# Reordering the mixes, the row factors and the last norm of a gated retention block on one core

## The chip, the cores and the metric

One NeuronCore of a Trainium2 chip runs the whole program. The metric is the device time of one execution in microseconds, lower is better. All tensors are float32; the large products run on fp32r operands that are split into a high and a low part.

## The reference, cut to what matters

The input x is (8, 1024, 128): eight sequences of 1024 tokens, 128 channels. A conditioning vector gives each sequence two scales, two shifts and two gates. A retention block (8 heads, keys of 64, values of 128, decay in place of a softmax) and then a token-shift feed-forward block are added to x.

```python
mod = (_silu(L0_c) @ L0_wmod).reshape(L0_c.shape[0], 6, 1, -1)
sa, ca, ga, sb, cb, gb = (mod[:, 0], mod[:, 1], mod[:, 2], mod[:, 3], mod[:, 4], mod[:, 5])
...
h = _layernorm(x, axis=-1) * (1 + ca) + sa
x = x + ga * _L0_attn_ref(h, ...)
h = _layernorm(x, axis=-1) * (1 + cb) + sb
x = x + gb * _L0_ffn_ref(h, ...)
return x
...
# in _L0_attn_ref: q, k rotated; scores times decay; then
o = jnp.einsum('bhts,bhsv->bhtv', scores, v)
o = (o - mean) * jax.lax.rsqrt(var + EPS)
o = o * gn_weight.reshape(H, V) + gn_bias.reshape(H, V)
o = o * jax.nn.silu(g)
return jnp.einsum('btc,oc->bto', o, Wo)
...
# in _L0_ffn_ref
xr = mu_r * x + (1.0 - mu_r) * x_prev
xk = mu_k * x + (1.0 - mu_k) * x_prev
r = jax.nn.sigmoid(jnp.einsum('btc,dc->btd', xr, W_r))
k_act = jnp.square(jax.nn.relu(jnp.einsum('btc,dc->btd', xk, W_k)))
out = r * jnp.einsum('btc,dc->btd', k_act, W_v)
```

## The kernel before, in words

The 8192 tokens are cut into 64 chunks of 128; four chunks are a group of 512 tokens, so there are 16 groups, numbered 0 to 15 (LAST is 15). Each engine has its own instruction stream, written out by hand: a prologue for the first chunks and then one loop over `steps`, in which every piece of work has an own offset (`due(step - 11, GC, LAST)` means: in step 11, 15, 19 and so on, for group 0, 1, 2). Inside an engine the order of the lines is the order of the work; between engines there are semaphores alone. The step numbers of different engines are not the same moment: VectorE's step t follows ScalarE's step t - 1.

One step carries one chunk through TensorE: `turn_heads` and `transpose_k`, `attend`, `scores`, `recall`, `state`, and projections of later chunks. TensorE's PSUM banks are a ring of five; a bank is taken only when the reader of its last content has released it, so TensorE waits for VectorE's products of rotated keys and queries (`sin_k`, `cos_q`), for the states (`S`) and for ScalarE's copies (`v`). `recall` ends a chunk's heads; ScalarE squares them (`square`, tile N), VectorE sums the squares (`sum_squares`, gn_sum), GpSimd makes 1/std (`head_rstd`, a power of -0.5), VectorE normalises (`norm_heads`), and the next `attend` but one needs the heads' banks free again. GpSimd also finishes the rotations (`rotate_k`, `rotate_q`) and multiplies two heads a step by their gates (`gate_head`, tile y).

Once in four steps, a group's work is added to that:
- From group 4 on (BY_ROWS) the first norm is made on the turned input: `apply_rows` (VectorE, line 1071) multiplies x_turned by the row factors 1/std and by the channel scale, and `add_rows` (GpSimd, line 1410) adds the row of shifts. Before, apply_rows stands between the two halves of `norm_heads`, and add_rows ahead of `rotate_k`.
- The feed-forward's token shift: `mix_delta` (GpSimd, line 1461) makes h minus its predecessor, `mix_shift_r` (line 1164) and `mix_shift_k` (line 1170, in place, tile delta) on VectorE make both mixes, and `round_mix` (ScalarE, line 847) the high part of mix k. Before, both mixes stand ahead of the masks of the scores (`mask`, line 1125), and round_mix is the last line of ScalarE's step.
- The norms' statistics: `norm_stats` (VectorE, lines 1051 and 1054) is four bn_stats and four bn_aggr; `norm_rstd` on GpSimd makes 1/std and the shift.

The end is written out for group 15 in two halves of 256 tokens: `last_residual`, `last_stats`, `last_rstd` (GpSimd), `last_apply` (ScalarE, line 864), `last_transpose` (TensorE, with `keep_busy` matmuls of no use ahead of each half), `last_modulate` (ScalarE, line 884), `last_mix` (VectorE, line 1232), `last_k`, `last_r`, `last_ffn` (TensorE), and `last_product`. GpSimd's last line is `ffn_out` of group 14, whose store SP waits for before it issues the last two.

Of the kernel before, what the change touches and what calls it, by code (L numbers as in the profile page):

```python
# [9 lines left out]
ALU = mybir.AluOpType  # L10
# [39 lines left out]
    "last_heads", "last_k_act", "last_k_psum", "last_mix_k", "last_mix_r", "last_mv", "last_n1T", "last_neg",  # L50
    "last_out", "last_product", "last_r_psum", "last_r_tanh", "last_relu", "last_residual", "last_rstd",
    "last_scaled", "last_shift", "last_stats", "last_var", "last_y", "ln_apply0", "ln_apply1", "ln_mv0",
# [39 lines left out]
def build(nc, x, xT, cT, w_mod, w_qkT, w_gT, w_vT, w_oT, norm_wb, w_ffnT, ffn_mu, const, const_q, out):  # L92
    with ExitStack() as ctx:
# [201 lines left out]
        def _(e):  # L295
# [427 lines left out]
        def _(e):  # L723
# [135 lines left out]
            def last_apply(part):  # L859
                at.wait_ge("last_shift", part + 1)  # L860
                at.wait_ge("n0T", BY_ROWS)
                at.wait_ge("n1T", LAST)
                for j in range(GC)[chunks_of(part)]:
                    e.activation(normed[:, j, :], X[:, LAST % NX, j, :], ACT.Identity, bias=ln_shift[:, 1, j:j + 1],
                                 scale=ln_rstd[:, 1, j:j + 1]).then_inc(sem["last_apply"])

# [83 lines left out]
            for step in steps:  # L950
                for i in due(step, 1, NCHUNK, 4):
                    square(i, 0)
                for i in due(step, 1, NCHUNK, 4):
                    square(i, 1)
                for g in due(step - 12, GC, LAST - 1):
                    act_r(g)
# [28 lines left out]
                for g in due(step - 9, GC, LAST):  # L985
                    round_mix(g)
# [5 lines left out]
            last_apply(0)  # L992
            last_modulate(0)
            last_apply(1)
            last_modulate(1)
            for part in range(PARTS):
                last_relu(part)
                last_act_r(part)

        @block.vector  # L1000
        def _(e):
# [42 lines left out]
            def norm_stats(g, which):  # L1044
# [4 lines left out]
                at.wait_ge(f"ln_shift{which}", g)  # L1049
                for j in range(GC):  # L1050
                    e.bn_stats(ln_stats[:, which, j, :], X[:, g % NX, j, :]).then_inc(sem[f"ln_stats{which}"])
                for j in range(GC):
                    at.wait_ge(f"ln_stats{which}", GC * g + j + 1)
                    done = e.bn_aggr(ln_mv[:, which, j, :], ln_stats[:, which, j, :])
# [152 lines left out]
            def last_stats(part):  # L1207
# [10 lines left out]
                at.wait_ge("last_mv", part + 1)  # L1218
                e.tensor_scalar(ln_neg[:, 1, these], ln_mv[:, 1, these, 0], -1.0, None, ALU.mult).then_inc(sem["last_neg"])

            def last_mix(part):
# [9 lines left out]
                for n, what in ((1, "k"), (0, "r")):  # L1231
                    e.scalar_tensor_tensor(out=last_mixed[what][:, cols], in0=last_delta[:, cols], scalar=mu[:, n:n + 1], in1=before,
                                           op0=ALU.mult, op1=ALU.add).then_inc(sem["last_mix_" + what])
# [17 lines left out]
            norm_stats(0, 0)  # L1251
            sum_w_v()
# [11 lines left out]
            norm_stats(1, 0)  # L1264
            mask(0, 1)
            mask(0, 0)
            add_state(0)
            rotate_k(2)
# [24 lines left out]
            norm_stats(3, 0)  # L1293
            norm_heads(2, 0)
# [9 lines left out]
            for step in steps:  # L1304
# [4 lines left out]
                for g in due(step + 10, GC, NGROUP, 4):  # L1309
                    norm_stats(g, 0)  # L1310
                for g in due(step - 11, GC, LAST):
# [3 lines left out]
                for g in due(step - 11, GC, LAST):  # L1315
                    mix_shift_k(g)
                for g in due(step - 9, GC, LAST):
                    norm_stats(g, 1)
                for i in due(step, 1, NCHUNK, 5):
# [376 lines left out]
```

## Time and profile before

| | us |
|---|---|
| three timed runs | 750.21, 751.33, 752.49 (median 751.33) |
| the profiled execution | 750.83 |
| its span, first to last instruction | 749.0 |
| TensorE busy | 735.4 |
| VectorE busy | 605.7 |
| GpSimd busy | 604.3 |
| ScalarE busy | 482.4 |

The profile is of one execution. Busy times of TensorE overlap a little, because matmuls are pipelined and their ends are modelled; a stall of TensorE is seen more exactly in the distance between the starts of two matmuls. A row of the timeline gives the start, the duration, engine, line and tiles, and in brackets how long the engine was idle before it and what it then waited for. Rows that follow one another closely are merged (x2).

### The profile page before, as it was taken

The numbers are of one execution on the slowest core, as the hardware profiler recorded it, in microseconds if no ns is written. First come the engines' busy times: TensorE is split into PE (matmuls) and PEld (weight loads), VectorE is DVE, ScalarE is ACT, GpSimd is POOL, SyncE is SP. The second block draws the span as 40 slices with busy tenths as digits, with TensorE's granted clock in tenths as the row PEclk, the third lists the DMA queues.
The fourth block names the chain that finished last, engine by engine and source line by source line (L and its number), as shares of the span: only waits on it lengthen the run. The fifth ranks groups of instructions, "written<-read, shape, count | busy, mean of one in ns | idle before, by whom it ended". The sixth has DMA issues, their size and how long they took to land.

```text
span 749.0 us, 29004 instructions
## 1 busy us (share of the span) xinstructions
PE 735.4 (98%) x12123; PEld 643.0 (86%) x12123; DVE 605.7 (81%) x1265; ACT 482.4 (64%) x932; POOL 604.3 (81%) x655
## 2 busy tenths in 40 slices
PE   8989999999999999999999999999999999999997
PEld 7778888888889889888888988988888888988886
DVE  4997688878888887988888898887898878787546
ACT  4566666575665666666666665766666666656665
POOL 5877779789698897988889797888979889787641
PEclk9999999999999999999999999999999999999999
DMA  7611020200202121030211303021020201001001
GB/s 249 193 31 20 13 59 10 65 18 16 79 17 79 25 73 30 10 93 13 75 25 26 81 13 87 9 79 31 13 84 17 73 16 30 18 9 31 24 15 29
DMA packets 59809, 35.15 MB, mean 47 GB/s; under 512 B 36664, under 2 KB 54432, under 8 KB 59680
## 3 DMA queue, kind: packets, MB, share of 16 engines
q1 hardware_dynamic: 58960, 32.51, 16.8%
q8 instruction: 96, 1.57, 0.9%
q10 hardware_dynamic: 720, 0.80, 0.3%
q14 instruction: 33, 0.27, 0.1%
HBM read 20.66 MB, written 4.25 MB: 33 GB/s over the span
## 4 chain that ended last, share of the span: by engine, by line
PE 81%; DVE 10%; issue 3%; ACT 2%; POOL 2%; DMA 1%; SPq 0%; DVEq 0%
PE ring L332 45%; PE outs L332 13%; PE O_E L332 12%; PE ring L347 7%; PE O_O L332 2%; DVE gn_sum L1145 2%; DVE N L1152 1%; DVE delta L1170 1%; ACT N L803 1%; DVE S L1139 1%; DMA N<-in_w_vT 1%; PE ring L397 1%; DVE mix_r L1164 1%; DVE rot_k L1115 1%; DVE sin_k L1118 1%
## 5 line engine op out<-in xcount | busy, mean ns | idle before, releaser
L1452 POOL TENSOR_TENSOR y<-y,gate 128x512 f32<-128x512 f32 x120 | 152.4, 1287 | 29.4 <-ACT y L815 29.4
L1435 POOL TENSOR_TENSOR rot_k<-rot_k,sin_k 128x256 f32<-128x256 f32 x128 | 106.2, 850 | 26.5 <-DVE sin_k L1118 25.8
L332 PEld LDWEIGHTS outs<-wo_gated,y 128*128 128x128 f32 x992 | 119.8, 192 | 6.7 <-DVE y L1191 0.5
L779 ACT ACTIVATE v<-ring 64x512 f32<-64x512 f32 x128 | 76.0, 594 | 75.3 <-PE ring L332 74.3
L332 PE MATMUL outs<-wo_gated,y 128*128 128x128 f32 x992 | 121.7, 275 | 0.1
L1145 DVE TENSOR_REDUCE gn_sum<-N 128x4 f32<-128x512 f32 x118 | 75.5, 681 | 43.4 <-ACT N L803 43.4
L1445 POOL TENSOR_TENSOR gn_rstd<-gn_var,minus_half 128x8 f32<-128x8 f32 x64 | 105.3, 1645 | 5.0
L787 ACT ACTIVATE kT<-ring 128x512 f32<-128x512 f32 x64 | 38.3, 598 | 103.0 <-PE ring L347 103.0
L815 ACT ACTIVATE y<-ring,gn 128x512 f32<-128x512 f32 x126 | 90.9, 777 | 5.2 <-PE ring L347 5.2
L1125 DVE TENSOR_TENSOR A<-ring,consts 128x256 f32<-128x256 f32 x128 | 48.2, 417 | 56.2 <-PE ring L332 56.2
L1429 POOL TENSOR_TENSOR qT<-qT,swapped 128x512 f32<-128x512 f32 x60 | 77.2, 1287 | 14.8 <-DVE swapped L1101 14.6
L808 ACT ACTIVATE gate<-ring 128x512 f32<-128x512 f32 x128 | 76.8, 601 | 3.6 <-PE ring L332 1.2
L1139 DVE TENSOR_TENSOR S<-ring,S 128x512 f32<-128x512 f32 x112 | 76.8, 685 | 2.9 <-PE ring L332 1.0
L332 PE MATMUL O_E<-v,A 64*64 64x128 f32 x992 | 68.0, 275 | 0.6 <-DVE N L1152 0.6
L332 PE MATMUL O_O<-v,A 64*64 64x128 f32 x992 | 68.0, 275 | 0.0
L332 PE MATMUL ring<-v,rot_k 64*64 64x128 f32 x960 | 67.5, 270 | 0.3 <-DVE A L1125 0.3
L332 PE MATMUL ring<-v,k_odd 64*64 64x128 f32 x960 | 67.1, 269 | 0.0
L332 PE MATMUL O_E<-S,qT 64*64 64x128 f32 x928 | 65.3, 269 | 0.1
L332 PE MATMUL O_O<-S,qT 64*64 64x128 f32 x928 | 64.6, 269 | 0.0
L332 PEld LDWEIGHTS ring<-v,rot_k 64*64 64x64 f32 x960 | 57.6, 133 | 0.8 <-issue 0.8
L332 PEld LDWEIGHTS ring<-v,k_odd 64*64 64x64 f32 x960 | 57.9, 133 | 0.0
L332 PEld LDWEIGHTS O_E<-v,A 64*64 64x64 f32 x992 | 53.1, 132 | 4.8 <-DVE N L1152 0.7
(199 smaller groups left out, 2107.9 us busy)
## 6 DMA issues: line engine op xcount, KB each, us to landing
k_odd<-rot_k SPq DMA_DIRECT2D x128, 64.0 KB, 2.2
row_of<-written_rows SPq DMA_DIRECT2D x12, 512.0 KB, 4.0
X<-in_x SPq DMA_DIRECT2D x16, 256.0 KB, 4.3
out<-X SPq DMA_DIRECT2D x15, 256.0 KB, 2.4
x_turned<-in_xT SPq DMA_DIRECT2D x12, 256.0 KB, 4.4
key_tables<-in_const SPq DMA_DIRECT2D x7, 256.0 KB, 5.1
rotary_q<-in_const_q SPq DMA_DIRECT2D x2, 512.0 KB, 6.4
gates<-stored_rows SPq DMA_DIRECT2D x8, 128.0 KB, 3.1
```

What stands on the lines that cost most here:

```text
L332: return e.matmul(o, lhsT, rhs, start=start, stop=stop, skip_group_check=True)
L347: done = e.transpose(bank[:, at_column:at_column + HALF], tokens[rows, :], ident[rows, rows])
L779: done = e.activation(v[halves(half), i % 2, 1, :, :], by(PAIRS, bank_of["v", odd, i][halves(1 - half), :]), ACT.Copy)
L808: e.activation(gate[:, n % 2, :], bank_of["gate", n][:, :], ACT.Silu).then_inc(sem["gate"])
L815: e.activation(in_halves(by(GC, y[:, n % NY, :])), from_halves(bank_of["n", n // 2], n % 2, GC), ACT.Identity, bias=gn[:, 1, h:h + 1], sca ...
L1125: e.tensor_tensor(A[:, odd, :, :], by(PAIRS, bank_of["kT", i][:, odd, W // 2:W]), causal.unsqueeze(1).broadcast_to([P, PAIRS, HALF]), ALU. ...
L1139: e.tensor_tensor(new, added, old, ALU.add).then_inc(sem["S"])
L1145: e.tensor_reduce(gn_sum[:, i % 2, odd, :], N[:, i % NN, odd, :, :], AXIS.X, ALU.add).then_inc(sem["sum_" + eo])
L1429: e.tensor_tensor(q, q, swapped[:, :], ALU.add).then_inc(sem["qT"])
L1435: done = e.tensor_tensor(turned[:, n, :, :], turned[:, n, :, :], sin[:, n, :, :], op)
L1445: e.tensor_tensor(gn_rstd[:, i % 2, :, :].rearrange("p e a -> p (e a)"), gn_var[:, i % 2, :, :].rearrange("p e a -> p (e a)"), minus_half[ ...
L1452: e.tensor_tensor(y[:, n % NY, :], y[:, n % NY, :], gate[:, n % 2, :], ALU.mult).then_inc(sem["y"])
```

## The change

- VectorE's `norm_stats` is cut into `norm_stats` (bn_stats) and `norm_mv` (bn_aggr). For group 2, in the prologue, the first part moves ahead of `rotate_k(2)`; both masks of chunk 2 move ahead of the second half of `norm_heads(0)`.
- In the loop, `mix_shift_k` and `apply_rows` move behind the masks, `round_mix` moves from the end of ScalarE's step to behind the squares of the next one, and GpSimd's `add_rows` moves between the two `gate_head`.
- At the end, `last_apply` moves from ScalarE to VectorE as (x - mean) * 1/std, so -mean and the shift are not made any more; mix k of both halves comes ahead of mix r; `last_k` of both halves comes first on TensorE, `last_relu` of both on ScalarE; the filler matmuls go from 5 and 4 to 2 and 3; `ffn_out` of group 14 moves from GpSimd to VectorE (`last_ffn_out`).

```diff
@@ TensorE
             at.wait_ge("n_O", NCHUNK)
-            keep_busy(O[1][:, :, :].rearrange("p n v -> p (n v)"), 5, True)
+            keep_busy(O[1][:, :, :].rearrange("p n v -> p (n v)"), 2, True)
             last_transpose(0)
-            keep_busy(O[1][:, :, :].rearrange("p n v -> p (n v)"), 4, True)
+            keep_busy(O[1][:, :, :].rearrange("p n v -> p (n v)"), 3, True)
             last_transpose(1)
             last_k(0)
+            last_k(1)
             last_r(0)
-            last_k(1)
@@ ScalarE
                 for i in due(step, 1, NCHUNK, 4):
                     square(i, 1)
+                for g in due(step - 10, GC, LAST):
+                    round_mix(g)
...
-                for g in due(step - 9, GC, LAST):
-                    round_mix(g)
...
             last_edge()
-            last_apply(0)
             last_modulate(0)
-            last_apply(1)
             last_modulate(1)
             for part in range(PARTS):
                 last_relu(part)
+            for part in range(PARTS):
                 last_act_r(part)
@@ VectorE
-                at.wait_ge("last_mv", part + 1)
-                e.tensor_scalar(ln_neg[:, 1, these], ln_mv[:, 1, these, 0], -1.0, None, ALU.mult).then_inc(sem["last_neg"])
+            def last_apply(part):
+                at.wait_ge("last_rstd", part + 1)
...
+                for j in range(GC)[chunks_of(part)]:
+                    e.tensor_scalar(normed[:, j, :], X[:, LAST % NX, j, :], ln_mv[:, 1, j, 0:1], ln_rstd[:, 1, j:j + 1],
+                                    ALU.subtract, ALU.mult).then_inc(sem["last_apply"])
...
             mask(0, 0)
             add_state(0)
+            norm_stats(2, 0)
             rotate_k(2)
...
             norm_heads(0, 0)
-            norm_heads(0, 1)
             mask(2, 1)
             mask(2, 0)
+            norm_heads(0, 1)
             rotate_q(5)
             add_state(2)
-            norm_stats(2, 0)
+            norm_mv(2, 0)
...
                     mix_shift_r(g)
...
-                for g in due(step - 11, GC, LAST):
-                    mix_shift_k(g)
...
                 for i in due(step, 1, NCHUNK, 5):
                     mask(i, 0)
+                for g in due(step - 11, GC, LAST):
+                    mix_shift_k(g)
+                for g in due(step + 6, GC, NGROUP, BY_ROWS):
+                    apply_rows(g)
                 for i in due(step - 1, 1, NCHUNK, 5):
                     sum_squares(i, 0)
...
-                for g in due(step + 6, GC, NGROUP, BY_ROWS):
-                    apply_rows(g)
...
             last_stats(1)
+            last_apply(0)
             ffn_product(LAST - 1)
+            last_apply(1)
             last_mix(0)
             last_mix(1)
+            last_mix_r(0)
             last_square(0)
+            last_mix_r(1)
             last_square(1)
+            last_ffn_out()
             last_product(0)
             last_product(1)
@@ GpSimd
-                at.wait_ge("last_rstd", part + 1)
-                at.wait_ge("last_neg", part + 1)
-                e.tensor_tensor(ln_shift[:, 1, these], ln_neg[:, 1, these], ln_rstd[:, 1, these], ALU.mult
-                                ).then_inc(sem["last_shift"])
...
-                for g in due(step + 8, GC, NGROUP, BY_ROWS):
-                    add_rows(g)
                 for i in due(step + 4, 1, NCHUNK, 7):
                     rotate_k(i)
...
                     gate_head(2 * i)
+                for g in due(step + 8, GC, NGROUP, BY_ROWS):
+                    add_rows(g)
                 for g in due(step - 11, GC, LAST - 1):
                     ffn_out(g)
...
             last_rstd(0)
             last_rstd(1)
-            ffn_out(LAST - 1)
```

## Rows read from the trace of the kernel before

**Rows 1.** The page, part 1: busy us (share of the span) xinstructions.
```profile
PE 735.4 (98%) x12123; PEld 643.0 (86%) x12123; DVE 605.7 (81%) x1265; ACT 482.4 (64%) x932; POOL 604.3 (81%) x655
```

**Rows 2.** Busy time by stage: stage, length, PE, PEld, DVE, ACT, POOL, clock, DMA, GB/s.
```profile
128.00:690.00 562.00, 561.52 (x9540) 495.01 (x9530) 470.96 (x963) 366.79 (x659) 479.64 (x507) 1.00 0.17 41
...
744.00:747.00 3.00, 1.71 (x13) 1.49 (x12) 2.03 (x5) 0.77 (x2) 0.00 (x0) 1.00 0.11 32
```

**Rows 3.** Waits of the weight loads, whole span: us in total, times, longest.
```profile
PEld ring L332 <- DVE S L1139: 3.6, 10, 0.5
PEld ring L332 <- ACT v L779: 3.6, 8, 1.0
```

**Rows 4.** Timeline of VectorE at the start: start us, us, engine, line, tiles.
```profile
27.30 0.69 DVE L1115 TENSOR_TENSOR rot_k<-ring,key_tables 128x512 f32<-128x512 f32 x1 [0.74 <-PE ring L332]
...
41.60 0.86 DVE L1051 BATCH_NORM_STATS2 ln_stats<-X 128x6 f32<-128x128 f32 x4
...
43.23 0.68 DVE L1098 TENSOR_TENSOR qT<-ring,rotary_q 128x512 f32<-128x512 f32 x1
```

**Rows 5.** Timelines of VectorE, GpSimd and TensorE, first group with row factors.
```profile
123.61 1.57 DVE L1071 SCALAR_TENSOR_TENSOR h_full<-x_turned,mod_cols,row_of 128x512 f32<-128x512 f32 x1
...
126.30 0.67 DVE L1118 TENSOR_TENSOR sin_k<-ring,key_tables 128x512 f32<-128x512 f32 x1
...
123.60 1.04 POOL L1461 TENSOR_TENSOR delta<-h2T 128x512 f32<-128x512 f32 x1
...
127.08 0.47 PE L347 MATMUL ring<-consts,rot_k 64*128 64x64 f32 x8 [0.99 <-issue]
```

**Rows 6.** Timelines of GpSimd, VectorE, ScalarE and TensorE in a regular group.
```profile
207.03 1.29 POOL L1452 TENSOR_TENSOR y<-y,gate 128x512 f32<-128x512 f32 x1 [1.30 <-ACT y L815]
...
216.58 1.73 POOL L1410 TENSOR_TENSOR h_full<-h_full,row_of 128x512 f32<-128x512 f32 x1
...
208.65 1.28 DVE L1145 TENSOR_REDUCE gn_sum<-N 128x4 f32<-128x512 f32 x2 [0.75 <-ACT N L803]
209.85 1.40 DVE L1139 TENSOR_TENSOR S<-ring,S 128x512 f32<-128x512 f32 x2
...
217.21 1.65 DVE L1170 SCALAR_TENSOR_TENSOR delta<-delta,mu,h2T 128x512 f32<-128x512 f32 x1
...
218.90 0.63 ACT L847 ACTIVATE mix_k_hi<-delta 128x512 fp32r<-128x512 f32 x1 [0.58 <-DVE delta L1170]
...
210.96 0.40 PE L332 MATMUL ring<-wv_hi,hT_hi 128*128 128x512 f32 x1
...
221.24 0.40 PE L332 MATMUL ring<-hT_lo,wg_hi 128*128 128x512 f32 x1
221.48 0.40 PE L332 MATMUL ring<-hT_hi,wg_lo 128*128 128x512 f32 x1
221.98 0.50 PE L332 MATMUL ring<-wv_hi,hT_hi 128*128 128x512 f32 x1
222.32 0.39 PE L332 MATMUL ring<-wv_lo,hT_hi 128*128 128x512 f32 x1
```

**Rows 7.** Timelines of VectorE, GpSimd and ScalarE at the end.
```profile
706.88 1.28 DVE L1145 TENSOR_REDUCE gn_sum<-N 128x4 f32<-128x512 f32 x2 [0.75 <-ACT N L803]
...
738.58 0.69 DVE L1185 SCALAR_TENSOR_TENSOR delta<-mix_r,ring 128x512 f32<-128x512 f32 x1
...
746.26 0.42 DVE L1249 TENSOR_TENSOR X<-X,h_full 128x256 f32<-128x256 f32 x1
...
738.67 0.69 POOL L1475 TENSOR_TENSOR ln_rows<-ln_var,minus_half 128x2 f32<-128x2 f32 x1
...
740.41 0.87 ACT L864 ACTIVATE normed<-X,ln_rows 128x128 f32<-128x128 f32 x2
741.70 0.57 ACT L884 ACTIVATE h2T<-ring,mod_cols 128x256 f32<-128x256 f32 x1 [0.42 <-PE ring L548]
```

**Rows 8.** Line 1170, mix_shift_k, whole span: ns min/median/max.
```profile
L1170 DVE SCALAR_TENSOR_TENSOR delta<-delta,mu,h2T x15: 748/1106/1650, 128.1 to 731.2; 128x512 f32<-128x512 f32 x15
```

More of the change, by code:

```diff
@@ L857, in load_tables @@
                 e.dma_start(key_tables[:, c, :, :, :].rearrange("p k h d -> p (k h d)"), columns).then_inc(sem[tables(c)[0]], 16)
[L859 to L865, printed above, removed]
             def last_scale(part):
@@ L1048, in norm_stats, with norm_mv @@
                     at.wait_ge("residual", g + 1)
-                at.wait_ge(f"ln_shift{which}", g)
+                at.wait_ge(f"ln_mv{which}", g)
                 for j in range(GC):
                     e.bn_stats(ln_stats[:, which, j, :], X[:, g % NX, j, :]).then_inc(sem[f"ln_stats{which}"])
+            def norm_mv(g, which):
+                at.wait_ge(f"ln_shift{which}", g)
                 for j in range(GC):
@@ L1217, in last_stats @@
                 done.then_inc(sem["last_mv"])
-                at.wait_ge("last_mv", part + 1)
-                e.tensor_scalar(ln_neg[:, 1, these], ln_mv[:, 1, these, 0], -1.0, None, ALU.mult).then_inc(sem["last_neg"])
+            def last_apply(part):
+                at.wait_ge("last_rstd", part + 1)
+                at.wait_ge("n0T", NGROUP)
+                at.wait_ge("n1T", LAST)
+                for j in range(GC)[chunks_of(part)]:
+                    e.tensor_scalar(normed[:, j, :], X[:, LAST % NX, j, :], ln_mv[:, 1, j, 0:1], ln_rstd[:, 1, j:j + 1],
+                                    ALU.subtract, ALU.mult).then_inc(sem["last_apply"])
             def last_mix(part):
@@ L1230, in last_mix, with last_mix_r, last_ffn_out @@
                 at.wait_ge("last_delta", part + 1)
-                for n, what in ((1, "k"), (0, "r")):
-                    e.scalar_tensor_tensor(out=last_mixed[what][:, cols], in0=last_delta[:, cols], scalar=mu[:, n:n + 1], in1=before,
-                                           op0=ALU.mult, op1=ALU.add).then_inc(sem["last_mix_" + what])
+                e.scalar_tensor_tensor(out=last_mixed["k"][:, cols], in0=last_delta[:, cols], scalar=mu[:, 1:2], in1=before,
+                                       op0=ALU.mult, op1=ALU.add).then_inc(sem["last_mix_k"])
+            def last_mix_r(part):
+                cols = tokens_of(part)
+                e.scalar_tensor_tensor(out=last_mixed["r"][:, cols], in0=last_delta[:, cols], scalar=mu[:, 0:1],
+                                       in1=h2T[:, 1, cols], op0=ALU.mult, op1=ALU.add).then_inc(sem["last_mix_r"])
+            def last_ffn_out():
+                xg = X[:, (LAST - 1) % NX, :, :]
+                at.wait_ge("product", LAST)
+                at.wait_ge("ffn_out", LAST - 1)
+                e.tensor_tensor(xg, xg, product, ALU.add).then_inc(sem["ffn_out"])
             def last_square(part):
@@ L1251, in _ @@
             norm_stats(0, 0)
+            norm_mv(0, 0)
             sum_w_v()
@@ L1264, in _ @@
             norm_stats(1, 0)
+            norm_mv(1, 0)
             mask(0, 1)
@@ L1293, in _ @@
             norm_stats(3, 0)
+            norm_mv(3, 0)
             norm_heads(2, 0)
@@ L1310, in _ @@
                     norm_stats(g, 0)
+                    norm_mv(g, 0)
                 for g in due(step - 11, GC, LAST):
@@ L1314, in _ @@
                     last_gate(2 * NCHUNK - 4)
-                for g in due(step - 11, GC, LAST):
-                    mix_shift_k(g)
                 for g in due(step - 9, GC, LAST):
                     norm_stats(g, 1)
+                    norm_mv(g, 1)
                 for i in due(step, 1, NCHUNK, 5):
```

4 lines of the change are left out of this document (2 added, 2 removed).

## The prediction

> **What bounds the kernel now.** I read the page's engine table first: TensorE is busy for 98% of the span [rows 1]. Then the busy times by stage: between 128 and 690 us TensorE is busy for 561.52 of 562 us at a granted clock of 1.00 [rows 2]. The long middle is therefore paid by TensorE's own work, and an edit on another engine can earn there only what TensorE still waits. Third, the waits: of TensorE's weight loads ten are for the running state S and eight for the copied values v [rows 3]. Matmul ends are modelled and overlap, so I measure a stall as the distance between two starts. Last I read the timelines at those places, by engine: the start [rows 4], the first group of four chunks [rows 5], one regular group [rows 6], and the end, where TensorE no longer sets the pace [rows 7].
>
> **The statistics in two parts.** At the start VectorE is the engine without gaps. The third group's statistics (four bn_stats from 41.60, 0.86 us, and four aggregations) stand ahead of the rotation whose cosine product at 43.23 frees the bank that TensorE waits for until its next transposes of keys [rows 4]. The change puts the four bn_stats ahead of rotate_k(2), where VectorE is idle for 0.74 us [rows 4]; the aggregations stay. So 0.86 us leave the busy stretch and 0.12 come back. The two masks that now go ahead of half of a normalisation may have to wait for their scores; no row of before shows that wait. It costs between 0 and 0.68 us, the length of a VectorE instruction of that size (the one at 43.23) [rows 4]. I take 0.3, near the middle, as no row is nearer to either end. Saved: 0.86 - 0.12 - 0.3 = 0.44, **0.45 us**, bounds 0.05 and 0.74. What is late next there is still VectorE, so the shift is carried on.
>
> **The product with the row factors (apply_rows) behind the masks.** In the first group it takes 1.57 us, since GpSimd's mix_delta, started at 123.60, reads SBUF beside it: 123.60 + 1.04 = 124.64, and VectorE ends 0.54 later [rows 5]. The key rotation behind it ends at 126.97, and TensorE resumes at 127.08 after 0.99 us of idle time, marked "issue" [rows 5]: it waited for the bank that this rotation frees. With apply_rows a stage earlier, the rotation ends about 1.5 us sooner and the whole wait goes: **1.0 us**, once. In later groups the same instruction did not stop TensorE, so there it saves nothing.
>
> Its new place costs something. Behind the masks it meets GpSimd's product of a gated head (207.03 to 208.32) [rows 6]. Both engines' pairs of SBUF operands exclude one another: mix_shift_k, 0.75 us at its shortest [rows 8], took 1.65 from 217.21, as GpSimd's row sum ran until 218.31; it ended 0.55 behind it, and the row sum itself had been stretched to 1.73 [rows 6]. So apply_rows will end near 208.32 + 0.55 = 208.87, and the sums of squares start 0.2 us later than 208.65. The first state S would end near 210.75 and not 210.53 (209.85 plus half of its pair), while TensorE needs it at 210.96 [rows 6]. Cover is 0.4 us and 0.2 of it is used: I cost it at nothing. If that cover were gone, each tenth of a microsecond would cost 1.2 us over 12 groups. GpSimd loses 0.55 here, and gets most of it back where the row sum no longer meets mix_shift.
>
> **mix_shift_k and round_mix moved.** In the regular group ScalarE stands idle for 0.58 us ahead of round_mix, until mix_shift_k is done, rounds from 218.90 to 219.53, and only then squares the heads [rows 6]. So sums, S and TensorE are late: the matmul at 221.98 starts 0.50 behind its predecessor at 221.48, and the next follows after 0.34 (222.32), where 0.24 is usual (221.24 to 221.48) [rows 6]. That is 0.26 + 0.10 = 0.36 us. Ten waits for S are two each in five such groups [rows 3]: 1.8 us. In the six groups between, the wait is for v, and ScalarE's delay is the same one: 3.6 us / 8 = 0.45 us of load wait [rows 3], about half of which moves matmuls, 0.2 each, 1.2 us in all. With round_mix behind the squares, ScalarE squares as soon as the heads are there. Against it: mix_shift_k now meets GpSimd's key rotation or, later, its gated head, and stands ahead of the sums. I expect it at about 218.6, freed by the end of the rotation, done near 219.4, so that the sums can start there, about 0.6 us earlier than behind a square that itself begins at 219.5. Of 3.0 us I take **1.7**, nearly all of the five and little of the six. Bounds: 3.0 saved, and 1.3 lost (0.25 in each of five groups) if GpSimd's head comes first. The row sum between two gated heads is only an order: GpSimd's work stays, and who waits for the later head is TensorE some 3 us afterwards.
>
> **The end.** Near the end of the loop the new order works against us: mix_shift_k for the last regular group ended before the masks; it will now stand ahead of the sums at 706.88 [rows 7], beside a gated head on GpSimd, and delay them by about 0.15 us (0 to 0.5), and the end is a chain of VectorE, GpSimd and TensorE, so this is paid: **-0.15**.
>
> After the last residual, ScalarE normalises the second half only at 740.41, though its 1/std was ready at 739.36 (738.67 + 0.69) [rows 7]: it was held by the first half's modulation. On VectorE there is neither the negation nor the last product with -mean, and the second half follows ffn_product (738.58, 0.69 us) [rows 7]: it starts near 739.4 and ends near 739.85, two 128x128 instructions priced at 0.45 us together. That lies between 0.34 (twice a quarter of the 0.68 us of 512 columns on VectorE) [rows 4] and 0.87 (the same two on ScalarE) [rows 7], nearer to the row of its own engine. Before it ended at 741.28. The second modulation then starts near 740.4 and not 741.70 [rows 7], 1.3 us earlier. The shorter runs of filler matmuls (5 to 2, 4 to 3) only have to be gone by then. Of this 1.3, VectorE takes some back: mix r of both halves comes behind mix k of both, and ffn_out(14), on GpSimd 1.29 us that nobody waited for (the length of a product of this size there, 207.03) [rows 6], becomes about 0.68 on VectorE [rows 4], ahead of the last products. My walk through VectorE's queue (difference, mix k, mix r, square of both halves, the added sum, two products) ends the last add 0.8 us earlier than 746.26 + 0.42 [rows 7]. The store of group 14 moves from about 741 to about 744.3, ahead of the two last stores on SP's queue; I give it 0 to 0.4 us. Taken: **0.8 us**, bounds 0.2 and 1.2.
>
> **Sum.** 0.45 + 1.0 + 1.7 - 0.15 + 0.8 = 3.8 us. The profiled execution took 750.83 us (span 749.0), 0.5 below the median of 751.33. 750.83 - 3.8 = **747.0 us**.
>
> **Rivals.**
> *Gated head first.* GpSimd's first gated head begins before mix_shift_k gets to its operands; mix_shift_k then ends near 220.3, the sums are 0.25 later than now, and the 1.7 turns into a loss of 1.3. For it: the two instants lie within 0.1 us in my walk. Against: GpSimd is still rotating keys then, later than before rather than earlier. 750.83 - 3.8 + 1.7 + 1.3 = 750.0 (748.7, if the five groups only stay as they are).
> *Port lost for two instructions (the slower side).* apply_rows in its new place gets its operands not behind the first GpSimd instruction but behind the next one too, 1.25 us later. The sums then start near 210.1; from 209.05 on (0.4 past 208.65) TensorE waits, so about 0.85 us in each of 12 groups: 10 us, 747.0 + 10 = 757. Against it: mix_shift_k got in between two back-to-back GpSimd instructions (row sum to 218.31, key rotation behind it) [rows 6].
> *The clock falls at the end.* Fewer filler matmuls might let TensorE drop from 2.4 to 1.2 GHz. The rows show 1.00 even in 744 to 747 us, where TensorE is busy for 1.71 of 3 us [rows 2], so I hold it unlikely. At the lower level those 1.71 us would take up to twice as long: 748.7. The Trainium skill ("TensorE: Matmul & The Clock Gate", What's actually happening) says that the throttled state is the default and activity releases it, which speaks against taking filler away; the trace shows no throttled stretch to test it on.
> *The end gives nothing.* The added sum and the late store eat the 0.8 us: 747.8.
>
> **How the numbers follow.** Forecast 0.58 (by itself 745.3 to 748.5), gated head first 0.20, two instructions 0.07, clock 0.05, no gain at the end 0.10. A measurement of this kernel can tell about 0.3%, 2.25 us, from no change. Faster: forecast and the last rival, and a little of the first, 0.70; same 0.22; slower 0.08. The range reaches from 745.0 (all bounds of the two larger savings met) to 750.6 (first rival with a poor end).
>
> **What would show it.** Right: TensorE's 0.99 us at 127 gone; weight loads no longer waiting for S in the loop; ScalarE's round_mix behind the squares and without a wait ahead of them; apply_rows about 1.0 to 1.3 us long just behind the masks; bn_stats in the gap at 26.5; the last normalisation at about 738.3 and 739.4 on VectorE. Wrong: new waits of TensorE for S, v or normalised heads in every group, or a last chain as long as before.

## The result, and the profile after

The changed kernel took 746.43 us (median of six runs, 746.32 to 747.75), the kernel before 751.23 (six runs beside it): a ratio of 0.994 with an interval of 0.993 to 0.9951, 4.8 us faster. The forecast was 747.0 (745.0 to 750.6). The profiled execution took 747.0, its span 745.2 us where before it was 749.0. The page's first part gives busy us, share of the span and instructions (PE is TensorE, PEld its weight loads, DVE VectorE, ACT ScalarE, POOL GpSimd):

```profile
PE 732.8 (98%) x12119; PEld 643.9 (86%) x12119; DVE 604.6 (81%) x1268; ACT 480.6 (64%) x928; POOL 607.5 (82%) x652
```

To see where the time went I take TensorE's timeline and the first matmul of every `attend` (tile O_E from v and A); the distance of two such starts is one step. The span is read to a tenth of a microsecond, so a stretch that ends with it is good to 0.05. Stretches between them, in us:

| stretch of before (us of its span) | before | after | difference | forecast |
|---|---|---|---|---|
| start to the first attend, 0 to 28.51 | 28.51 | 29.05 | +0.54 | 0 |
| first four steps, to 83.11 | 54.60 | 54.42 | -0.18 | -0.45 |
| next four, to 127.47 | 44.36 | 43.24 | -1.12 | -1.0 |
| the loop from the first group with row factors, to 703.74 | 576.27 | 574.08 | -2.19 | -1.7 |
| one step, to 711.68 | 7.94 | 8.05 | +0.11 | +0.15 |
| the end, to 749.0 | 37.32 | 36.36 | -0.96 | -0.8 |
| sum | 749.0 | 745.2 | -3.8 | -3.8 |

Most rows are near their forecast, but that doesn't show yet that the reasons were right. In the long middle TensorE no longer waits for S (3.6 us in ten waits before, [rows 3]). Busy times of that stage, as in [rows 2], and under them the waits of the weight loads in it (us in total, times, longest), in the changed kernel and, for v, in the same stretch of before:

```profile
128.00:690.00 562.00, 562.00 (x9523) 497.64 (x9514) 471.33 (x965) 368.65 (x665) 484.80 (x508) 1.00 0.17 41
```

```profile
PEld ring L332 <- issue: 8.8, 51, 0.2
PEld ring L332 <- ACT v L779: 2.3, 7, 0.3
```

```profile
PEld ring L332 <- ACT v L779: 2.6, 7, 0.4
```

TensorE's matmuls of the rotated keys at the first group with row factors start without a wait (0.99 us before, [rows 5]), and `apply_rows` in a later group takes 1.05 us in its new place:

```profile
126.36 0.41 PE L347 MATMUL ring<-consts,rot_k 64*128 64x64 f32 x8
...
207.21 1.05 DVE L1065 SCALAR_TENSOR_TENSOR h_full<-x_turned,mod_cols,row_of 128x512 f32<-128x512 f32 x1
```

One regular group, timelines of GpSimd, VectorE and ScalarE (start, duration, engine, line, operation, tiles; in brackets the idle time before), to be read beside [rows 6]:

```profile
215.14 1.27 POOL L1450 TENSOR_TENSOR qT<-qT,swapped 128x512 f32<-128x512 f32 x1
216.37 1.87 POOL L1456 TENSOR_TENSOR rot_k<-rot_k,sin_k 128x256 f32<-128x256 f32 x2
218.21 1.74 POOL L1473 TENSOR_TENSOR y<-y,gate 128x512 f32<-128x512 f32 x1
219.90 1.30 POOL L1431 TENSOR_TENSOR h_full<-h_full,row_of 128x512 f32<-128x512 f32 x1
...
215.22 1.74 DVE L1158 SCALAR_TENSOR_TENSOR mix_r<-delta,mu,h2T 128x512 f32<-128x512 f32 x1
217.28 0.76 DVE L1119 TENSOR_TENSOR A<-ring,consts 128x256 f32<-128x256 f32 x2 [0.32 <-PE ring L332]
217.95 0.84 DVE L1164 SCALAR_TENSOR_TENSOR delta<-delta,mu,h2T 128x512 f32<-128x512 f32 x1
218.79 1.28 DVE L1139 TENSOR_REDUCE gn_sum<-N 128x4 f32<-128x512 f32 x2
219.98 1.41 DVE L1133 TENSOR_TENSOR S<-ring,S 128x512 f32<-128x512 f32 x2
...
218.16 0.60 ACT L803 ACTIVATE N<-O_E 128x512 f32<-128x512 f32 x1 [0.46 <-PE O_O L332]
218.65 0.59 ACT L803 ACTIVATE N<-O_O 128x512 f32<-128x512 f32 x1
219.13 0.64 ACT L847 ACTIVATE mix_k_hi<-delta 128x512 fp32r<-128x512 f32 x1
```

ScalarE squares as soon as the heads are there (it now waits for TensorE, not for VectorE) and rounds behind that. mix_shift_k takes 0.84 us where it had 1.65, and this time GpSimd's gated head is the one that is stretched (1.74 instead of 1.29). mix_shift_r has become the long one (1.74); VectorE waits 0.32 us for TensorE behind it all the same.

The end, VectorE, TensorE and ScalarE:

```profile
735.31 0.60 DVE L1218 TENSOR_SCALAR normed<-X,ln_mv,ln_rows 128x128 f32<-128x128 f32 x2
735.83 0.68 DVE L1179 SCALAR_TENSOR_TENSOR delta<-mix_r,ring 128x512 f32<-128x512 f32 x1
736.43 0.60 DVE L1218 TENSOR_SCALAR normed<-X,ln_mv,ln_rows 128x128 f32<-128x128 f32 x2
...
740.60 0.69 DVE L1243 TENSOR_TENSOR X<-X,delta 128x512 f32<-128x512 f32 x1
...
742.45 0.42 DVE L1259 TENSOR_TENSOR X<-X,h_full 128x256 f32<-128x256 f32 x1
...
736.00 0.38 PE L548 MATMUL ring<-consts,normed 128*128 128x128 f32 x2
736.13 0.95 PE L332 MATMUL O_O<-wqk_hi 128*128 128x512 f32 x3
736.92 0.49 PE L548 MATMUL ring<-consts,normed 128*128 128x128 f32 x2
...
737.45 0.56 ACT L876 ACTIVATE h2T<-ring,mod_cols 128x256 f32<-128x256 f32 x1 [0.47 <-PE ring L548]
```

The two normalisations lie on both sides of the product, as forecast; a pair took 0.60 us, not 0.45. The last add ends at 742.87, 3.81 us earlier than in [rows 7] (746.68), of which 2.84 had been gained before the end began (711.68 against 708.84).

### The profile page after: what moved, and what is told of

Its sections match the earlier page's. It is cut to its first block, busy times and chain, and to the rows that moved or that the text cites. A ratio compares the mean times of both kernels' runs of the same rounds, so it can differ in the third digit from the quotient of the medians.

```text
span 745.2 us, 29021 instructions
## 1 busy us (share of the span) xinstructions
PE 732.8 (98%) x12119; PEld 643.9 (86%) x12119; DVE 604.6 (81%) x1268; ACT 480.6 (64%) x928; POOL 607.5 (82%) x652
## 4 chain that ended last, share of the span: by engine, by line
PE 92%; DVE 3%; POOL 2%; ACT 1%; issue 1%; DMA 1%; SPq 0%; DVEq 0%
PE ring L332 51%; PE outs L332 15%; PE O_E L332 14%; PE ring L347 8%; PE O_O L332 3%; PE ring L397 1%; DMA N<-in_w_qkT 1%; POOL gn_rstd L1466 0%; ACT normed L751 0%; POOL y L1473 0%; ACT y L815 0%; DVE N L1146 0%; DVE A L1119 0%; DVE qT L1080 0%; POOL rot_k L1456 0%
## 5 line engine op out<-in xcount | busy, mean ns | idle before, releaser
L1473 POOL TENSOR_TENSOR y<-y,gate 128x512 f32<-128x512 f32 x120 | 158.8, 1337 | 29.4 <-ACT y L815 29.4
L1456 POOL TENSOR_TENSOR rot_k<-rot_k,sin_k 128x256 f32<-128x256 f32 x128 | 102.6, 822 | 26.9 <-DVE sin_k L1112 25.6
L1146 DVE TENSOR_TENSOR N<-O_E,gn_rstd 128x512 f32<-128x512 f32 x62 | 42.4, 684 | 24.2 <-POOL gn_rstd L1466 24.1
```

The source lines that it names most:

```text
L1456: done = e.tensor_tensor(turned[:, n, :, :], turned[:, n, :, :], sin[:, n, :, :], op)
L1473: e.tensor_tensor(y[:, n % NY, :], y[:, n % NY, :], gate[:, n % 2, :], ALU.mult).then_inc(sem["y"])
```

## The experiments

All twelve in one table first. "Median" is the change of the median against the runs of before beside it (these were 751.19 for the first four kernels, 750.88 for the next four, 750.94 for the last), with the interval of the ratio. The other columns are from the one profiled execution: from the first attend to the end of the span (before 720.49 us), and five steps. "127" is the step that ends at the first group with row factors, "first" the step after it, "odd" and "even" the first step of such a group (at 216 and 261 us), "end" the stretch from the last attend on. The odd groups are the five whose first step is like that at 216 us, the even ones the six between them.

| kernel | median, us | ratio | from attend | 127 | first | odd | even | end |
|---|---|---|---|---|---|---|---|---|
| before | 0 | 1 | 0 | 11.95 | 10.43 | 10.82 | 10.65 | 37.32 |
| changed | -4.80 | 0.993 to 0.9951 | -4.34 | 10.75 | 10.62 | 10.43 | 10.56 | 36.36 |
| e1 mixes alone | -2.04 | 0.9966 to 0.9986 | -1.74 | 11.95 | 10.87 | 10.43 | 10.57 | 37.34 |
| e2 apply_rows and add_rows | -2.67 | 0.9954 to 0.9979 | -2.32 | 10.75 | 10.59 | 10.65 | 10.57 | 37.34 |
| e3 end alone | -1.07 | 0.9976 to 0.9993 | -1.34 | 11.95 | 10.42 | 10.83 | 10.63 | 36.35 |
| e4 statistics alone | -0.59 | 0.9986 to 1.0004 | -0.87 | 11.95 | 10.41 | 10.83 | 10.65 | 37.36 |
| e5 apply_rows alone | +0.56 | 0.9999 to 1.0016 | +0.32 | 10.76 | 10.59 | 11.20 | 10.56 | 37.29 |
| e6 add_rows alone | -2.45 | 0.9948 to 0.9975 | -2.63 | 11.94 | 10.49 | 10.43 | 10.57 | 37.31 |
| e7 changed, round_mix back | +4.31 | 1.0036 to 1.0066 | +3.89 | 10.75 | 11.86 | 11.37 | 10.57 | 36.36 |
| e8 changed, mix_shift_k back | -4.69 | 0.9919 to 0.9947 | -5.04 | 10.75 | 10.60 | 10.43 | 10.55 | 36.32 |
| e9 e8 and masks back | -4.85 | 0.9917 to 0.9942 | -5.18 | 10.75 | 10.61 | 10.43 | 10.59 | 36.39 |
| e10 changed, more filler | -4.19 | 0.9929 to 0.9954 | -4.06 | 10.76 | 10.62 | 10.41 | 10.59 | 37.22 |
| e11 changed, sum on GpSimd | -3.53 | 0.9943 to 0.997 | -3.71 | 10.76 | 10.62 | 10.41 | 10.59 | 36.98 |
| e12 changed, add_rows back | -4.36 | 0.9927 to 0.9951 | -5.06 | 10.75 | 10.61 | 10.41 | 10.56 | 36.32 |

**One part at a time (e1 to e4).**

> The kernel before with one part alone: mix_shift_k behind the masks and round_mix behind the squares. Theory A (the prediction's): ScalarE's order is what pays, so this part alone gains 1.7 us less 0.15 at the end of the loop; between the profiled executions of before and after the loop's steps shrank by 2.2 us, so 1.5 to 2.2 us are expected, a ratio of 0.997 to 0.998, with odd groups 0.36 to 0.39 us shorter and no weight load that waits for S in the loop. Rival B: the row sum (add_rows) that no longer lies beside mix_shift_k is what pays (mix_shift_k took 1.65 us beside it and 0.84 in the changed kernel); then this part alone gains under 0.5 us and the next run gains the rest.

```diff
@@ ScalarE
                     square(i, 1)
+                for g in due(step - 10, GC, LAST):
+                    round_mix(g)
...
-                for g in due(step - 9, GC, LAST):
-                    round_mix(g)
@@ VectorE
-                for g in due(step - 11, GC, LAST):
-                    mix_shift_k(g)
...
                     mask(i, 0)
+                for g in due(step - 11, GC, LAST):
+                    mix_shift_k(g)
```

2.0 us, as theory A has it: the odd groups' wait is gone (10.82 to 10.43). Two waits for S are left, 0.6 us, both in the first group, whose step grew to 10.87.

> The kernel before with one part alone: apply_rows behind the masks and add_rows between the two gated heads. Theory A: 1.0 us once, at the first group with row factors (TensorE's 0.99 us at 127 us gone), nothing in the later groups: a ratio of 0.9985 to 0.9988. Rival B (the row sum out of mix_shift_k's way is what pays in the loop): 1.0 plus about 1.9, so near 0.996. Rival C (the port is lost for two instructions in some groups): new waits of TensorE for S, and a gain under 0.5 us or a loss.

```diff
@@ VectorE
                     mask(i, 0)
+                for g in due(step + 6, GC, NGROUP, BY_ROWS):
+                    apply_rows(g)
...
-                for g in due(step + 6, GC, NGROUP, BY_ROWS):
-                    apply_rows(g)
@@ GpSimd
-                for g in due(step + 8, GC, NGROUP, BY_ROWS):
-                    add_rows(g)
...
                     gate_head(2 * i)
+                for g in due(step + 8, GC, NGROUP, BY_ROWS):
+                    add_rows(g)
```

2.7 us, where theory A had 1.0. The step before 127 gave its 1.2, but the odd groups shrank too. So neither theory holds as it stands. By the steps from 83 us to the last but one attend, e1 gained 1.66 us and e2 2.34, together 4.0; the changed kernel, with both, has 3.3 there. In part the two take away the same wait. (One step of that stretch, from 505.60 us of before on, differs without any edit that would explain it: it took 12.33 us in before, 12.59 in e1, 12.10 in e2 and 12.11 in the changed kernel. Without it the gains are 1.92, 2.12 and 3.09, so the conclusion stays.)

> The kernel before with the end alone: last norm on VectorE, mix k ahead of mix r, fewer filler matmuls, the last sum of group 14 on VectorE. Theory A: 0.8 to 1.0 us, all of it between the last attend and the end of the span: a ratio near 0.9988. Rival B: the end of the changed kernel was shorter because the loop before it handed over earlier; then this part alone gains under 0.5 us.

The edit is the change's part for the end alone. Its core is shown; the shorter runs of filler matmuls, TensorE's and `last_relu`'s order and the functions themselves are as in the change:

```diff
@@ ScalarE
-            last_apply(0)
             last_modulate(0)
-            last_apply(1)
             last_modulate(1)
@@ VectorE
+            last_apply(0)
             ffn_product(LAST - 1)
+            last_apply(1)
...
+            last_mix_r(0)
             last_square(0)
+            last_mix_r(1)
             last_square(1)
+            last_ffn_out()
@@ GpSimd
-            ffn_out(LAST - 1)
```

1.07 us, and in the profile the end is 0.97 us shorter: theory A.

> The kernel before with the third group's statistics in two parts and both masks of chunk 2 ahead of half a normalisation. The prediction had 0.45 us; the profile of the changed kernel shows 0.2 us less between 28.5 and 83 us, and a new stall of TensorE of 0.71 us at 40.6. Theory A (this part's gain is real and small): 0.2 us, a ratio of 0.9995 to 1.0. Rival B: as predicted, 0.45 us. Rival C: a loss, since rotate_q(5) now stands behind the masks and half a normalisation.

```diff
             add_state(0)
+            norm_stats(2, 0)
             rotate_k(2)
...
             norm_heads(0, 0)
-            norm_heads(0, 1)
             mask(2, 1)
             mask(2, 0)
+            norm_heads(0, 1)
             rotate_q(5)
             add_state(2)
-            norm_stats(2, 0)
+            norm_mv(2, 0)
```

0.59 us by the medians, with an interval that takes in zero; in the profile the first two steps fall from 33.69 to 33.20 us, 0.49, which is B, the prediction's own size. The changed kernel has the same two steps at 33.23. That its first four steps gained only 0.18 comes from a later pause: between two state matmuls at 75.42 and 75.99 TensorE stood still with no releaser in the trace ("issue"), and that step, the fourth, took 10.87 us. It takes 10.61 in before and e9, 10.59 in e2, 10.73 in e11, and 10.41 or 10.42 in the other nine, so the pause isn't the change's; what makes it stays open. TensorE of the changed kernel there:

```profile
75.99 0.27 PE L332 MATMUL ring<-v,k_odd 64*64 64x128 f32 x1 [0.30 <-issue]
```

**Which half of e2 pays (e5, e6).**

> The kernel before with apply_rows alone behind the masks; add_rows stays ahead of the key rotation. The two together gained 2.7 us where I had 1.0. Theory A: apply_rows gives the single wait at the first group with row factors (the step ahead of it 11.95 to 10.75 us) and nothing in the later groups, whose odd ones stay at 44.67 us: 1.2 us, 0.9984. Rival B: its new place pays in each group too: 2.4 us or more.

> The kernel before with add_rows alone between the two gated heads; apply_rows stays. Theory A: the row sum no longer lies beside mix_shift_k, which falls from 1.65 to 1.1 us, so ScalarE's rounding and squares come 0.5 us sooner and the odd groups shrink from 44.67 to about 44.52, the even ones by 0.05: about 1.1 us, while the wait of 0.99 us at 127 us stays. Rival B: a mere order, as I predicted: under 0.3 us.

e5's edit is the part of e2's for VectorE, e6's the part for GpSimd:

```diff
@@ VectorE (e5)
                     mask(i, 0)
+                for g in due(step + 6, GC, NGROUP, BY_ROWS):
+                    apply_rows(g)
@@ GpSimd (e6)
                     gate_head(2 * i)
+                for g in due(step + 8, GC, NGROUP, BY_ROWS):
+                    add_rows(g)
```

Neither theory held. add_rows alone gave 2.45 us, more than either had, the whole gain of the loop (odd 10.43, as in the changed kernel); apply_rows alone took the wait at 127 away, 1.2 us, as theory A has it, but lost more than that in the loop (odd 11.20, 0.38 over before), which neither had. First one row of GpSimd in before, then e5, then e6: GpSimd, VectorE, ScalarE, and of e5 TensorE.

```profile
208.26 1.31 POOL L1466 TENSOR_TENSOR X<-X,delta 128x512 f32<-128x512 f32 x1
```

```profile
205.82 1.28 POOL L1452 TENSOR_TENSOR y<-y,gate 128x512 f32<-128x512 f32 x1 [1.30 <-ACT y L815]
207.06 1.75 POOL L1466 TENSOR_TENSOR X<-X,delta 128x512 f32<-128x512 f32 x1
...
214.52 1.28 POOL L1429 TENSOR_TENSOR qT<-qT,swapped 128x512 f32<-128x512 f32 x1
215.75 1.73 POOL L1410 TENSOR_TENSOR h_full<-h_full,row_of 128x512 f32<-128x512 f32 x1
...
206.61 1.04 DVE L1071 SCALAR_TENSOR_TENSOR h_full<-x_turned,mod_cols,row_of 128x512 f32<-128x512 f32 x1
...
214.60 1.75 DVE L1164 SCALAR_TENSOR_TENSOR mix_r<-delta,mu,h2T 128x512 f32<-128x512 f32 x1
216.39 1.65 DVE L1170 SCALAR_TENSOR_TENSOR delta<-delta,mu,h2T 128x512 f32<-128x512 f32 x1
...
218.07 0.63 ACT L847 ACTIVATE mix_k_hi<-delta 128x512 fp32r<-128x512 f32 x1 [0.97 <-DVE delta L1170]
...
220.27 0.40 PE L332 MATMUL ring<-hT_hi,wg_lo 128*128 128x512 f32 x1
221.15 0.50 PE L332 MATMUL ring<-wv_hi,hT_hi 128*128 128x512 f32 x1 [0.48 <-DVE S L1139]
```

```profile
215.88 2.34 POOL L1435 TENSOR_TENSOR rot_k<-rot_k,sin_k 128x256 f32<-128x256 f32 x2
...
215.36 1.12 DVE L1164 SCALAR_TENSOR_TENSOR mix_r<-delta,mu,h2T 128x512 f32<-128x512 f32 x1
216.51 1.11 DVE L1170 SCALAR_TENSOR_TENSOR delta<-delta,mu,h2T 128x512 f32<-128x512 f32 x1
...
217.65 0.63 ACT L847 ACTIVATE mix_k_hi<-delta 128x512 fp32r<-128x512 f32 x1
218.19 0.58 ACT L803 ACTIVATE N<-O_E 128x512 f32<-128x512 f32 x1
```

In e6 mix_shift_k meets the key rotation instead of the row sum, takes 1.11 us and not 1.65, and ScalarE's rounding and squares begin earlier, though in the old order and without a wait. In e5 apply_rows got its operands 0.55 us behind the end of the gated head (207.10 to 207.65) and in turn stretched GpSimd's next sum to 1.75 us (1.31 in before). GpSimd is then 0.4 us later against TensorE; mix_shift_k still ends 0.56 behind the row sum (217.48 to 218.04), as it did in [rows 6], and so all of it is 0.4 later: ScalarE waits 0.97 instead of 0.58, and TensorE starts 0.88 us behind its predecessor (220.27 to 221.15) instead of 0.50.

**Which half of the mixes pays (e7, e8).**

> The changed kernel with round_mix put back to the end of ScalarE's step, mix_shift_k still behind the masks. Theory A: ScalarE's order is what pays; the rounding then waits for mix_shift_k (done at 218.8 in the regular group) with the squares behind it, so these begin near 219.4 and not 218.2, and the odd groups return to 44.67 us or more: 2 to 4 us slower than the changed kernel, 748.5 to 750.5 us. Rival B: mix_shift_k's place is what pays: within 0.5 us of the changed kernel.

> The changed kernel with mix_shift_k put back ahead of the masks, round_mix still behind the squares. Theory A: ScalarE's order is what pays, VectorE's has slack: within 0.5 us of the changed kernel (746.0 to 747.0 us), odd groups at 44.3 to 44.35 us. Rival B: mix_shift_k's place pays: 1.5 to 2.5 us slower, odd groups above 44.5 us and waits for S again.

```diff
@@ ScalarE (e7)
-                for g in due(step - 10, GC, LAST):
-                    round_mix(g)
...
+                for g in due(step - 9, GC, LAST):
+                    round_mix(g)
@@ VectorE (e8)
                     last_gate(2 * NCHUNK - 4)
+                for g in due(step - 11, GC, LAST):
+                    mix_shift_k(g)
...
                     mask(i, 0)
-                for g in due(step - 11, GC, LAST):
-                    mix_shift_k(g)
```

ScalarE's order pays, theory A in both. With mix_shift_k back ahead of the masks the loop is that of the changed kernel, and the step of 8.05 us near its end is 7.94 again: the forecast's loss there. With round_mix back the kernel is 8.8 us slower than the changed one, more than the 2 to 4 I expected: ScalarE now waits 1.13 us for the late mix with the squares behind it, and the weight loads' waits for S grow to 9.5 us. The odd groups lose 0.94 us each against the changed kernel, and other places lose as much or more: the first group 1.24, the group that starts at 662 us of before 1.15 (11.47 for 10.32), and the step near the end of the loop 1.27 (9.32 for 8.05). VectorE, ScalarE, and the waits from 128 to 690 us, of e7:

```profile
219.23 0.84 DVE L1164 SCALAR_TENSOR_TENSOR delta<-delta,mu,h2T 128x512 f32<-128x512 f32 x1
...
220.10 0.63 ACT L847 ACTIVATE mix_k_hi<-delta 128x512 fp32r<-128x512 f32 x1 [1.13 <-DVE delta L1164]
```

```profile
PEld ring L332 <- DVE S L1133: 9.5, 14, 1.4
```

**Whether the two cures stand alone (e12).**

> The changed kernel with add_rows alone put back ahead of the key rotation. Alone, add_rows between the gated heads gave the whole gain of the loop, and so did the order of the mixes. Theory A (either of the two takes the same wait away): with the mixes behind the masks and the rounding behind the squares the loop stays as in the changed kernel, odd groups at 44.3 us: within 0.5 us of it, 746.0 to 747.0 us. Rival B (add_rows is what pays and the mixes only did so where apply_rows stood in its old place): odd groups at 44.5 us or more, 747.5 us or more.

```diff
@@ GpSimd
+                for g in due(step + 8, GC, NGROUP, BY_ROWS):
+                    add_rows(g)
...
                     gate_head(2 * i)
-                for g in due(step + 8, GC, NGROUP, BY_ROWS):
-                    add_rows(g)
```

The loop is that of the changed kernel (odd 10.41): theory A. So the row sum's move and the mixes' order are two cures of one wait. With apply_rows in its old place either is enough (e6 and e1, odd 10.43). With apply_rows in its new one the order is enough (e12), while the row sum's move alone leaves 0.2 us in each odd group (e2, 10.65).

**The masks, the filler and the sum (e9 to e11).**

> The changed kernel with mix_shift_k ahead of the masks (as in the run before) and, in the prologue, the masks of chunk 2 back behind both halves of the first normalisation. Theory A: the moved masks cost a wait for scores, put at 0.3 us in the prediction, and the stall of TensorE of 0.71 us at 40.6; without them the stretch from the first attend to the third is 0.2 to 0.4 us shorter than the 33.2 to 33.3 us of the other runs with the split statistics, and the kernel 745.8 to 746.0 us. Rival B: the masks ahead are what frees TensorE (its scores' bank); without them that stretch is as long as before, 33.7 us.

```diff
             norm_heads(0, 0)
+            norm_heads(0, 1)
             mask(2, 1)
             mask(2, 0)
-            norm_heads(0, 1)
```

Theory A: the first two steps take 32.90 us where e8 has 33.31 and the other runs with the split statistics 33.20 to 33.23, one (e7) 33.53. In the first of the two steps, where the seven others agree best (15.56 to 15.59), e9 has 15.27. The moved masks cost 0.3 to 0.4 us. e9 has the lowest median of all, 746.09 (745.54 to 746.17), but its interval overlaps that of the changed kernel.

> The changed kernel with 5 and 4 filler matmuls again in place of 2 and 3. Theory A: the clock does not need them; in the changed kernel a filler takes about 0.24 us and the first transposes start at 736.00, right behind two of them and 0.1 us behind the normed rows, so three more push the first half by about 0.7 us and one more the second by about 0.9: the end is 0.7 to 0.9 us longer, 747.1 to 747.3 us. Rival B: fewer fillers slow TensorE's clock; then more of them gain 0.3 us or more, with a granted clock of 1.00 at 740 to 742 us where the changed kernel has less.

```diff
@@ TensorE
-            keep_busy(O[1][:, :, :].rearrange("p n v -> p (n v)"), 2, True)
+            keep_busy(O[1][:, :, :].rearrange("p n v -> p (n v)"), 5, True)
             last_transpose(0)
-            keep_busy(O[1][:, :, :].rearrange("p n v -> p (n v)"), 3, True)
+            keep_busy(O[1][:, :, :].rearrange("p n v -> p (n v)"), 4, True)
```

In the profile the end is 0.86 us longer (37.22 against 36.36): theory A. The granted clock is 1.00 from 738 to 742 us in the changed kernel, so there is nothing to win back. The medians show 0.3 us only. TensorE of e10:

```profile
734.89 1.40 PE L332 MATMUL O_O<-wqk_hi 128*128 128x512 f32 x5
736.12 0.38 PE L548 MATMUL ring<-consts,normed 128*128 128x128 f32 x2
736.26 1.18 PE L332 MATMUL O_O<-wqk_hi 128*128 128x512 f32 x4
737.27 0.38 PE L548 MATMUL ring<-consts,normed 128*128 128x128 f32 x2
```

> The changed kernel with the sum of group 14 back as GpSimd's last line. On VectorE it took 0.69 us at 740.60, ahead of the last products. Theory A: on GpSimd it starts behind the product of group 14, near 736.5, and lasts 1.3 us there, so it lies beside VectorE's first differences and mixes (two operands from SBUF) and holds up what is on the chain; what is saved at the products is paid there: within 0.3 us of the changed kernel. Rival B: the sum on VectorE is a plain cost; on GpSimd the end is 0.5 to 0.7 us shorter, 745.8 us.

```diff
@@ VectorE
-            last_ffn_out()
@@ GpSimd
             last_rstd(1)
+            ffn_out(LAST - 1)
```

Neither: it is slower, by 0.62 us in the end (36.98) and by 1.0 in the medians. The place of the damage was another than I had expected: the sum starts at 735.88, beside the second normalisation, and that takes 1.56 us instead of 0.60. GpSimd, VectorE and TensorE of e11:

```profile
735.88 1.31 POOL L1486 TENSOR_TENSOR X<-X,delta 128x512 f32<-128x512 f32 x1 [0.28 <-DVE delta L1179]
...
735.71 1.56 DVE L1218 TENSOR_SCALAR normed<-X,ln_mv,ln_rows 128x128 f32<-128x128 f32 x2
...
737.33 0.33 PE L548 MATMUL ring<-consts,normed 128*128 128x128 f32 x1 [0.85 <-DVE normed L1218]
```

So with the last norm on VectorE the sum at this place of GpSimd's queue costs more than it saves. Whether it pays to move it with the norm left on ScalarE was not run.

## Why the prediction was right, and where it was not

- **The statistics in two parts.** 0.45 forecast, 0.49 measured (e4, in one profile; by the medians 0.59, with an interval that takes in zero). The cost of the moved masks, for which I had only bounds (0 to 0.68) and took 0.3, is 0.3 to 0.4 (e9). Right, with its terms; that 0.3 came out of the middle of its bounds was luck.
- **apply_rows.** The wait at 127 is gone, 1.2 us for 1.0. What failed is "I cost it at nothing": I set the cost in VectorE's sums, which did have the cover, and let GpSimd "get most of it back". In the changed kernel the row sum does take 1.30 us where it took 1.73, but now the gated head ahead of it takes 1.74. The 0.44 us that GpSimd loses beside apply_rows (1.75 for 1.31) is paid where VectorE's mixes then wait for GpSimd to be done with the operands: 0.38 us in each odd group of e5 and 0.16 in the first group, more than the gain, and 0.22 in the odd groups of e2 (10.65 against 10.43 in e6). It doesn't show in the odd groups of the changed kernel because there the squares no longer stand behind the rounding; the first group's 0.19 us (10.43 to 10.62) remains.
- **The mixes.** 1.7 forecast, 1.64 measured in the loop of e1, 2.19 in that of the changed kernel; without the one step named at e2, which no edit explains, 1.89 and 1.97. The walk through VectorE's queue came out: I had mix_shift_k "at about 218.6" and "done near 219.4"; it ran from 217.95 to 218.79 in a group that began 0.61 us earlier than in before. The shares by group were right in sign: 0.39 in each odd group (I had 0.36), but 0.02 to 0.1 in the even ones, not 0.2. There "ScalarE's delay is the same one" failed: the loop's seven waits for v only fell from 2.6 to 2.3 us (the eighth of the eight that I divided by, 1.0 us, lies at the start of the kernel). The other step that failed is "the row sum between two gated heads is only an order: GpSimd's work stays". The row sum's place is what made mix_shift_k long, which I had read in [rows 6] (1.65 us, done 0.55 behind it) and used for apply_rows, but not here. Moved alone it gives all of the loop's gain (e6: 573.95 us from the start of the first group on, 576.27 before). The same 2 us stood behind two edits, and I put it down to one.
- **mix_shift_k.** In the changed kernel its own move earns nothing and costs 0.11 us near the end of the loop (e8), for which I had 0.15; what counts is that the rounding stands behind the squares. But the two can't be split the other way: with the late mix the rounding must be late too (e7).
- **The end.** 0.8 forecast, 0.96 measured. Inside it a pair of normalisations took 0.60 and not 0.45; the sum of group 14 on VectorE took 0.69, as I had it (0.68). The store of group 14 cost nothing: the span ends 2.3 us behind the last add in both kernels. The gain hangs on its parts together: with the old filler matmuls 0.10 of the 0.96 is left (e10), with the sum on GpSimd 0.34 (e11). How much of it the norm's new engine and how much the order of the mixes gives was not run.
- **The rivals.** "Gated head first" did not come in the odd groups, where it would have cost most: mix_shift_k (217.95) began 0.26 us ahead of the head (218.21). It did come in the first group with row factors and in the last three: there the head began 0.8 us ahead and mix_shift_k took 1.03 to 1.04 us, not 0.83 to 0.90. The price was small, 0.02 us in the first (10.62 against 10.60 in e8) and the 0.11 near the end of the loop. In e1's first group mix_shift_k took 1.38 us behind a head, and the step 10.87 instead of 10.43. The port lost for two instructions showed nowhere: apply_rows took 1.03 to 1.05 us in its new place. The clock did not fall at the end (1.00), and the end did give.

So the total was right partly because errors cancelled: the even groups gave less than I took, the single wait and the end more, and the profiled execution started 0.54 us later. The time came out closer than the gain: 747.0 forecast and 746.43 measured, but 3.8 us of gain forecast and 4.8 measured, because I counted from an execution (750.83) that was 0.4 us below the median of before.

## What to carry over

When two engines exclude each other over operands in SBUF, look for the pair of instructions that meet, and count how many edits of a change take away the wait that it causes: each may earn the whole gain alone, and together they earn it once. An instruction moved to where it meets another engine's work can cost that engine too, and the price appears at whoever waits for that engine next. Test the parts one by one even where the total came out as forecast.

## What the runs showed of the hardware

**One tensor from SBUF can be enough.** In e11 VectorE's second normalisation, two instructions that each read one tensor from SBUF and two columns of row factors, lay beside GpSimd's sum (735.88 to 737.19) and ended only 0.08 us behind it, at 737.27. This was seen once. I had expected that only of instructions with two tensors. The Trainium skill ("SBUF — State Buffer", Who interferes with whom) lists this form of instruction among those that can take the shared pair of ports in a two-port mode, and the trace agrees: 0.60 us alone, 1.56 beside GpSimd.

**The start isn't the same twice.** TensorE's granted clock over the first 20 us differs between executions of the same code there. Busy times by stage (PE, PEld, DVE, ACT, POOL, then the clock), first e8, then e12:

```profile
0.00:10.00 10.00, 8.46 (x45) 7.88 (x46) 2.95 (x14) 4.91 (x10) 4.73 (x13) 1.00 0.82 298
10.00:20.00 10.00, 9.13 (x44) 7.22 (x43) 7.42 (x12) 4.04 (x6) 7.82 (x7) 1.00 0.51 174
```

```profile
0.00:10.00 10.00, 7.44 (x40) 6.67 (x41) 2.96 (x14) 4.81 (x10) 4.57 (x13) 0.87 0.79 293
10.00:20.00 10.00, 10.00 (x43) 8.44 (x43) 5.89 (x10) 3.19 (x5) 6.44 (x7) 0.79 0.50 174
```

In e8 all is at the upper of the two levels (2.4 GHz) and the first attend is at 28.45 us; in e12 a part is at the lower one (1.2 GHz), with TensorE busy for 7.44 of the first 10 us instead of 8.46, and the first attend comes at 29.97. Over the 14 profiles that start lies between 28.14 and 29.97: between 28.14 and 28.55 in the five that have 1.00 throughout, between 28.32 and 29.97 in the nine with a part at the lower level. So the level alone doesn't settle the start. The spread is as large as most of the effects here, and the steps of the profile, which leave it out, tell the parts apart better than the medians; that the two columns differ by up to 0.7 us may be partly this.
